# Attention inside an adaLN block on one core: value products and row sums moved to a fixed distance behind the scores, rotary products moved from VectorE to GpSimd

## The reference, cut to what matters

```python
h = layernorm(x) * (1 + ca) + sa
q = rmsnorm(h @ wq_a.T) @ wq_b.T          # 32 heads of 64 (nope) + 64 (rotary)
ckv, k_pe = split(h @ wkv_a.T)            # 32 latent columns, 64 rotary columns
k_nope, v = split(rmsnorm(ckv) @ wkv_b.T)
q_pe, k_pe = rope(q_pe), rope(k_pe)       # even * cos - odd * sin, odd * cos + even * sin
p = softmax(causal(q_full @ k_full.T * scale))
x = x + ga * ((p @ v) @ wo.T)
x = x + gb * ffn(layernorm(x) * (1 + cb) + sb)   # silu(gate) * up, then down
```

## Time and profile before

| | |
|---|---|
| median of 3 runs | 863.45 us (863.05 to 864.19) |
| the profiled execution, its own time | 862.18 us |
| its span, first to last instruction | 860.4 us |
| mean granted TensorE clock | 0.958 of full speed |
| busy: PE, DVE, POOL, ACT | 785.7, 533.1, 327.7, 271.5 us |
| first scores of window 0 | at 140.49 us |
| first scores of window 7 | at 560.01 us |
| first output product (L662) | at 615.58 us |

### The profile page before, as it was taken

One profiled execution on the slowest core, in us unless ns is written; L12 is line 12 of the kernel. 1 busy time (PEld: TensorE's weight loads), 2 busy tenths in 40 slices (PEclk: granted clock), 3 DMA queues, 4 the chain that ended last, 5 costly groups with the idle time before them and its releaser, 6 DMA issues.

```text
span 860.4 us, 10667 instructions
## 1 busy us (share of the span) xinstructions
PE 785.7 (91%) x3968; PEld 531.4 (62%) x3968; DVE 533.1 (62%) x836; ACT 271.5 (32%) x402; POOL 327.7 (38%) x199
## 2 busy tenths in 40 slices
PE   5659597999998999999999999999799899999997
PEld 5658254564664655656656655544487688886886
DVE  3354484896896896987978977756465333222342
ACT  2360002333433433433343333343344332221220
POOL 9220022374574574484564663524344100000111
PEclk9895687999999999999999999999899899999999
DMA  8300714306107007016034057046000032220011
GB/s 343 114 0 1 158 52 98 64 1 131 32 0 161 2 2 161 1 32 132 1 70 93 1 106 262 2 147 220 1 1 0 1 111 74 73 65 1 24 38 37
DMA packets 30275, 60.49 MB, mean 70 GB/s; under 512 B 4656, under 2 KB 16688, under 8 KB 28432
## 3 DMA queue, kind: packets, MB, share of 16 engines
q1 hardware_dynamic: 29024, 57.11, 24.8%
q10 hardware_dynamic: 1200, 2.69, 0.8%
HBM read 32.40 MB, written 2.10 MB: 40 GB/s over the span
## 4 chain that ended last, share of the span: by engine, by line
PE 60%; issue 12%; DVE 8%; POOL 7%; SPq 4%; DMA 4%; ACT 3%; POOLq 0%; ACTq 0%; DVEq 0%
PE PS L691 14%; PE PS L585 7%; PE PS L530 6%; PE PS L662 5%; PE PS L588 5%; PE PS L586 5%; PE PS L601 4%; POOL PR L1389 3%; DMA Q<-TQ 3%; SPq L386 2%; PE PS L459 2%; PE PS L521 2%; PE PS L534 1%; POOL RE L1354 1%; PE PS L512 1%
## 5 line engine op out<-in xcount | busy, mean ns | idle before, releaser
L817 ACT ACTIVATE PR<-PS 128x1024 f32<-128x1024 f32 (+1 forms) x144 | 132.9, 929 | 262.1 <-PE PS L588 183.5
L1085 DVE TENSOR_REDUCE NMa<-PS 128x1 f32<-128x512 f32 (+3 forms) x216 | 140.3, 665 | 44.4 <-PE PS L534 29.0
L530 PE MATMUL PS<-KH,Q 96*128 96x512 f32 (+3 forms) x384 | 132.2, 400 | 12.7 <-DMA Q<-TQ 10.6
L585 PE MATMUL PS<-Q,KH 128*128 128x512 f32 x288 | 132.5, 460 | 3.7 <-DMA Q<-NM 2.6
L1389 POOL TENSOR_TENSOR PR<-PR 128x1024 f32<-128x1024 f32 (+3 forms) x56 | 119.8, 2139 | 27.9 <-ACT PR L817 24.1
L691 PE MATMUL PS<-Q 128*128 128x512 f32 (+1 forms) x528 | 123.2, 396 | 5.1 <-DVE Q L1253 4.5
L691 PEld LDWEIGHTS PS<-Q 128*128 128x128 f32 (+1 forms) x528 | 99.3, 189 | 28.1 <-DVE Q L1253 4.7
L588 PE MATMUL PS<-Q,KH 128*128 128x512 f32 x288 | 114.6, 398 | 0.0
L586 PE MATMUL PS<-Q,KL 128*128 128x512 f32 x288 | 114.3, 397 | 0.0
L530 PEld LDWEIGHTS PS<-KH,Q 96*128 96x128 f32 x384 | 71.9, 196 | 49.2 <-issue 20.1
L585 PEld LDWEIGHTS PS<-Q,KH 128*128 128x128 f32 x288 | 56.1, 195 | 60.1 <-issue 28.2
(11 more groups left out here) (161 smaller groups left out, 1084.4 us busy)
## 6 DMA issues: line engine op xcount, KB each, us to landing
Q<-TQ SPq DMA_DIRECT2D x96, 256.0 KB, 5.0
PR<-in_wmod SPq DMA_DIRECT2D x6, 1024.0 KB, 7.2
RT<-in_wo SPq DMA_DIRECT2D x4, 1024.0 KB, 4.9
TQ<-in_wo SPq DMA_DIRECT2D x4, 1024.0 KB, 4.9
WI<-in_gate_w SPq DMA_DIRECT2D x10, 256.0 KB, 3.2
WI<-in_up_w SPq DMA_DIRECT2D x10, 256.0 KB, 3.6
DI<-in_down_w SPq DMA_DIRECT2D x10, 256.0 KB, 3.6
TQ<-in_x ACTq DMA_DIRECT2D x2, 1024.0 KB, 10.3
```

The costliest lines, as they stand in the source:

```text
L530: ins = pe.matmul(bank[:, i * w:(i + 1) * w], M.Q[0:KR, g % 2, 0, h0 + i, qt * P:(qt + 1) * P], M.KH[0:KR, lo:lo + w], start=(i == 0), sto ...
L585: pe.matmul(dst, M.KH[:, ks], M.Q[:, w % 2, 0, :, qs], start=True, stop=False)
L817: act.activation(tiles, banks, ACT.Exp).then_inc(S_.p, 1)
L1085: dve.tensor_reduce(dst, PS[:, bank_of(turn), 0:n * w].rearrange("p (h k) -> p h k", k=w), axis=AX.X, op=ALU.max, negate=True).then_inc(S_ ...
```

## The change

- **Order.** `UNITS` lists the 36 blocks of a window; every engine walks them with one table of side work per block. The values of a step come 3 blocks behind its last block and its sum 2 blocks behind, across the boundary of windows: the last two steps of a window are multiplied and added in the first blocks of the next one. `join` stands behind block 30 and `rows` behind block 32 of 0 to 35; before, both stood behind block 34, right behind the last part.
- **Sums.** DVE adds all four heads in one instruction; POOL adds none.
- **Rotary products.** For groups 1 to 7 ACT copies the even and odd projections out of their banks into RT, and POOL forms the four products (`rotate_even`, `rotate_odd`) and then the two sums. The latent's high part is copied by ACT for every group; DVE keeps the subtraction. ACT's copy waits until the preceding half has been combined (`re`).
- **Halves.** Q is laid out by query half, the maxima parts of half 0 come first (parts 0 to 10), and queries are sent by half: 4 transfers of 96 partitions for each half, 8 for a group where 12 were. Half 0 of group w+2 is sent in window w; half 1 of group w+1 at the start of window w. The key's columns are interleaved to match. In the prologue half 0 of group 1 is sent ahead of group 0's maxima.
- **Rows.** The score products use 97, 96 and 96 rows instead of 128, and the zero rows (six of seven memsets at the start) go.
- **Banks.** One `free` semaphore for each of the three banks, since ACT now frees some of them.

The diff, cut to its core:

```diff
-    return sorted(parts, key=lambda part: part[3] + part[4])
+    return sorted(parts, key=lambda part: (part[0] >= NS // 2, part[3] + part[4]))
...
+UNITS = [(s, i) for s in range(NSTEP) for i in range(units_of(s))]
+NUNIT = len(UNITS)
+VALUE_LAG, ADD_LAG = 3, 2
+
+
+def due(n, lag):
+
+    return [((n - lag) // NUNIT * -1, s) for s in range(NSTEP) if UNITS.index((s, units_of(s) - 1)) == (n - lag) % NUNIT]
+
+
+VALUES = [due(n, VALUE_LAG) for n in range(NUNIT)]
+SUMS = [due(n, ADD_LAG) for n in range(NUNIT)]
+LATE_VALUES = [s for n in range(NUNIT) for ago, s in VALUES[n] if ago]
+LATE_SUMS = [s for n in range(NUNIT) for ago, s in SUMS[n] if ago]
...
-        self.side, self.free = sem("side_filled"), sem("side_free")
+        self.side, self.free = sem("side_filled"), [sem(f"side_bank{b}_free") for b in range(3)]
...
-        self.q = [sem(f"q_sent{h}") for h in range(HG)]
+        self.q = [[sem(f"q_half{hf}_sent{h}") for h in range(HG)] for hf in range(2)]
...
-QUERY_PLACES = [(0.13, ("w", 0), 0.5), (0.14, ("w", 1), 0.15), (0.15, ("w", 2), 0.15), (0.25, ("even", 0), 1.2),
-                (0.28, ("odd", 0), 1.2), (0.36, ("lat", 0), 1.3), (0.40, ("split", 0), 0.0),
-                (0.54, ("even", 1), 1.2), (0.57, ("odd", 1), 1.2), (0.65, ("lat", 1), 1.3), (0.75, ("split", 1), 0.0)]
-WINDOW_US = 56.0
+QUERY_PLACES = [(0.10, ("w", 0), 0.5), (0.105, ("w", 1), 0.15), (0.11, ("w", 2), 0.15), (0.20, ("even", 0), 0.0),
+                (0.23, ("odd", 0), 0.0), (0.30, ("lat", 0), 0.7), (0.43, ("split", 0), 0.0),
+                (0.46, ("even", 1), 0.0), (0.49, ("odd", 1), 0.0), (0.56, ("lat", 1), 0.7), (0.70, ("split", 1), 0.0)]
+WINDOW_US = 57.0
...
-    begin, end = 0.1, 0.80
+    begin, end = 0.04, 0.84
     places = [(begin + (end - begin) * sum(cost[:k]) / sum(cost), ("part", k), cost[k]) for k in range(len(PARTS))]
-    return places + [(end + 0.01, ("join",), 0.1), (end + 0.02, ("rows",), 0.3)]
+    return places + [(end + 0.02, ("join",), 0.1), (end + 0.06, ("rows",), 0.3)]
...
-        places += [(0.09, ("den", 1), 0.7), (0.10, ("inv", 1), 0.8), (0.17, ("norm", 1), 0.0)]
+        places += [(0.15, ("den", 1), 0.7), (0.16, ("inv", 1), 0.8), (0.24, ("norm", 1), 0.0)]
+    places += [(0.42, ("den", 0), 0.7), (0.43, ("inv", 0), 0.8), (0.50, ("norm", 0), 0.0)]
+    places.sort(key=lambda x: x[0])
+    table = []
+    free = 0.0
+    for n in range(NUNIT):
+        place = (n + 1) / NUNIT
+        for ago, s in SUMS[n]:
+            if s in ADDS:
+                free = max(free, place) + (HG * width(s) / 960 + 0.07) / WINDOW_US
+        names = []
+        while places and (n == NUNIT - 1 or max(places[0][0], free - SLACK) <= place):
+            _, name, busy = places.pop(0)
+            names.append(name)
+            free = max(free, place) + busy / WINDOW_US
+        table.append(names)
     return table
...
-    def send_queries(g):
-        sp.wait_ge(S_.tl, 2 * (g + 1))
+    def send_queries(g, hf):
+        cols = slice(hf * QB, hf * QB + QB)
+        sp.wait_ge(S_.tl, 2 * g + hf + 1)
         if g > 1:
-            sp.wait_ge(S_.sc, NEXP * (g - 1))
+            sp.wait_ge(S_.sc, NEXP * (g - 2) + (FIRST_EXP[4] if hf == 0 else NEXP))
         for h in range(HG):
-            for b in range(3):
-                sp.dma_start(M.Q[b * 32:(b + 1) * 32, g % 2, :, h, :].bitcast(F32),
-                             M.TQ[h * 32:(h + 1) * 32, b, :, :].bitcast(F32)).then_inc(S_.q[h], 16)
+            sp.dma_start(M.Q[0:KR, g % 2, :, hf, h, :].bitcast(F32),
+                         M.TQ[h * L:(h + 1) * L, :, :, cols].bitcast(F32)).then_inc(S_.q[hf][h], 16)
...
-    sp.wait_ge(S_.pads, 7)
-    send_queries(0)
+    sp.wait_ge(S_.one, 1)
+    send_queries(0, 0)
+    send_queries(0, 1)
     load_weights(1)
     load_mod(5)
+    send_queries(1, 0)
     send_maxima(0)
-    for w in range(G - 1):
+    for w in range(G):
         if w < G - 2:
             load_weights(w + 2)
-        send_queries(w + 1)
+        if w < G - 1:
+            send_queries(w + 1, 1)
+        if w < G - 2:
+            send_queries(w + 2, 0)
         if w == G - 2:
-            for h in range(HG):
...
-        send_maxima(w + 1)
+        if w < G - 1:
+            send_maxima(w + 1)
...
-            pe.wait_ge(S_.free, turn - 2)
+            pe.wait_ge(S_.free[turn % 3], turn // 3)
...
-            pe.wait_ge(S_.q[h0 + i], 48 * (g + 1))
-            ins = pe.matmul(bank[:, i * w:(i + 1) * w], M.Q[0:KR, g % 2, 0, h0 + i, qt * P:(qt + 1) * P],
+            pe.wait_ge(S_.q[qt // 4][h0 + i], 16 * (g + 1))
+            ins = pe.matmul(bank[:, i * w:(i + 1) * w], M.Q[0:KR, g % 2, 0, qt // 4, h0 + i, qs],
...
-        pe.matmul(dst, M.KH[:, ks], M.Q[:, w % 2, 0, :, qs], start=True, stop=False)
-        pe.matmul(dst, M.KL[:, ks], M.Q[:, w % 2, 0, :, qs], start=False, stop=False)
         diagonal = i == 0 and s in DIAGONALS
-        ins = pe.matmul(dst, M.KH[:, ks], M.Q[:, w % 2, 1, :, qs], start=False, stop=not diagonal)
+        pe.matmul(dst, M.KH[0:KR + 1, ks], M.Q[0:KR + 1, w % 2, 0, qb, :, qs], start=True, stop=False)
+        pe.matmul(dst, M.KL[0:KR, ks], M.Q[0:KR, w % 2, 0, qb, :, qs], start=False, stop=False)
+        ins = pe.matmul(dst, M.KH[0:KR, ks], M.Q[0:KR, w % 2, 1, qb, :, qs], start=False, stop=not diagonal)
...
-        for s in range(NSTEP + 1):
-            if s < NSTEP:
-                for i in range(units_of(s)):
-                    scores(w, s, i)
-                    for name in TABLES[w].get(("s", s, i), []):
-                        side(of_window(w, name))
-            if s == NSTEP:
-                for name in TABLES[w]["last"]:
-                    side(of_window(w, name))
-            if s > 0:
-                values(w, s - 1)
-                for name in TABLES[w].get(("v", s - 1), []):
-                    side(of_window(w, name))
-        for name in TABLES[w]["end"]:
-            side(of_window(w, name))
+        for n, (s, i) in enumerate(UNITS):
+            scores(w, s, i)
+            for ago, before in VALUES[n]:
+                if ago <= w:
+                    values(w - ago, before)
+            for name in TABLES[w][n]:
+                side(of_window(w, name))
+    for s in LATE_VALUES:
+        values(G - 1, s)
     denominator(G - 1, 1)
...
+    def queries_copied(kind, g, hf):
+        turn = TURN[(kind, g, hf)]
+        act.wait_ge(S_.side, turn + 1)
+        act.wait_ge(S_.re, 2 * (2 * g + hf))
+        act.activation(M.RT[:, ("even", "odd").index(kind), :], PS[:, bank_of(turn), :], ACT.Copy).then_inc(
+            S_.free[turn % 3], 1)
+
+    def latent_high(g, hf):
+        turn = TURN[("lat", g, hf)]
+        cols = slice(hf * 512, hf * 512 + 512)
+        if g > 0:
+            for h in range(HG):
+                act.wait_ge(S_.q[hf][h], 16 * g)
+        act.wait_ge(S_.side, turn + 1)
+        act.activation(M.TQ[:, 2, 0, cols], PS[:, bank_of(turn), :], ACT.Copy).then_inc(S_.lh, 1)
 
...
-                    side(of_window(w, name))
-            if s == 4:
-                empty(w, 0)
-        for name in TABLES[w]["end"]:
-            side(of_window(w, name))
-        empty(w, 1)
+        for n, (s, i) in enumerate(UNITS):
+            e = FIRST_EXP[s] + i // 2
+            if i + 1 == EXPS[e][1] + EXPS[e][2]:
+                exponentials(w, e)
+            for ago, before in VALUES[n]:
+                if ago <= w and before in (3, NSTEP - 1):
+                    empty(w - ago, STEPS[before][0])
+            for name in TABLES[w][n]:
+                side(of_window(w, name))
+    empty(G - 1, 1)
...
-        if hf == 0 and g > 0:
-            for h in range(HG):
-                dve.wait_ge(S_.q[h], 48 * g)
-        dve.wait_ge(S_.side, turn + 1)
-        dve.tensor_copy(M.TQ[:, 2, 0, cols], PS[:, bank_of(turn), :]).then_inc(S_.lh, 1)
         dve.wait_ge(S_.lh, 2 * g + hf + 1)
         dve.tensor_tensor(M.TQ[:, 2, 1, cols], PS[:, bank_of(turn), :], M.TQ[:, 2, 0, cols].bitcast(F32),
-                          ALU.subtract).then_inc(S_.free, 1)
...
         if NADD * w + j > 0:
-            dve.wait_ge(S_.ae, NADD * w + j)
-        sums = M.SUM[qb][:, POOL_HEADS:, QB - wd:QB]
-        dve.tensor_tensor(sums, sums, M.slot(s)[:, POOL_HEADS:, 0:wd], ALU.add).then_inc(S_.ae, 1)
+            dve.wait_ge(S_.ad, NADD * w + j)
+        sums = M.SUM[qb][:, :, QB - wd:QB]
+        dve.tensor_tensor(sums, sums, M.slot(s)[:, :, 0:wd], ALU.add).then_inc(S_.ad, 1)
...
+        for n in range(NUNIT):
+            for ago, s in SUMS[n]:
+                if ago <= w and s in ADDS:
+                    add(w - ago, s)
+            for name in TABLES[w][n]:
+                side(of_window(w, name))
+    for s in LATE_SUMS:
+        add(G - 1, s)
...
-    pads = [(M.KH[KR:, :], 0.0), (M.KL[KR:, :], 0.0), (M.KH[KR:KR + 1, :], 1.0)]
-    pads += [(M.Q[KR:, par, hl], 0.0) for par in range(2) for hl in range(2)]
-    for n, (rows, value) in enumerate(pads):
-        if n > 0:
-            pool.wait_ge(S_.pads, n)
```

(47 more changed lines are left out.)

211 lines of the change are left out of this document (74 added, 137 removed).

## The result

The changed kernel takes 864.72 us (median of 20 runs, 862.1 to 869.78), the kernel before 862.55 in as many: a ratio of 1.0036 with an interval of 1.0024 to 1.0047. It is slightly slower. The forecast was 838 with a range of 822 to 856.

What follows compares the result with a forecast made beforehand. PE, busy 785.7 of 860.4 us, was taken as the bound, so only its idle could be won. Prologue -10.0, boundaries -12.9 and end -1.3 made -24.2, from 862.2 to 838 us; range 822 to 856.

Steps and rivals of the forecast that it cites:

- DVE is then [44.6 to 50.5]: DVE's load per window, 44.6 us if it never waits, 50.5 if it waits as before; under PE's 58.4.
- rival of the held side banks: In the windows, DVE's long sums outlast three banks' 3.5 us cover, costing PE 0.5 each at four sums; 851 us, chance 0.17.
- the fall by 5: DVE's load per window falls by 5 us, an argument against PE waiting on side banks.
- ACT waits for POOL: Rival: in the windows ACT's copy waits for POOL's rotary chain, delaying exponentials and stopping PE; 871 us, chance 0.10.
- Prologue: Before window 0: earlier sends and less DVE work, -10 us in all, bounds -5 and -16.
- the early half: Prologue: half 0 of group 0 is sent 6.4 us earlier, so group 1's weights land at about 102.1; -6.4 us.
- The stretch behind it: Prologue, 108.50 to 137.90: DVE falls to 19.4 us, PE's 25.46 then bounds it; -3.9 us.
- Boundaries: Window boundaries: PE's idle mostly goes, -9.8 in windows 1 to 5, -1.8 window 0, -1.3 window 6; -12.9 us.
- the 0.3 kept: Windows 1 to 5: PE idle still left after the change, 0.3 us a window, 1.5 in five.
- End: Window 7 loses 0.5 of idle, and one DVE add replaces POOL's adds behind it, -0.8; together -1.3 us.
- Faster transfers: Rival: sends naming 96 partitions double the 208 GB/s, so prologue weights land 7 us sooner; 831 us, chance 0.10.
- costed at nothing: Edits priced at 0, among them 96- and 97-row score products, with up to 3 us either way in the range.

Runs made afterwards that it cites:

- experiment 12: Kernel of experiment 5 with the first send of group 0 held until both query halves are ready; 856.21 us, 0.9935 of the kernel before.
- experiment 5: Changed kernel with the low part of half 1 moved from behind block 25 to behind block 28; 848.25 us, 0.9826 of the kernel before.
- Experiment 11: Kernel of experiment 5 with join and rows both behind the last block instead of 30 and 32; 899.23 us, 1.0443 of the kernel before.
- experiment 2: Changed kernel with 128 rows again in all score products, zero rows written again; 853.18 us, 0.991 of the kernel before.
- 1: Changed kernel with the low part's table entry one block later, which left ACT's and POOL's order as it was; 864.9 us, 1.0047 of the kernel before.
- experiment 10: Changed kernel with the low part behind block 28 and 128 rows in the score products, no filler; 839.46 us, 0.9737 of the kernel before.
- experiment 9: Changed kernel with the low part behind block 28, 128 rows and 14 unread filler products ahead of window 0; 837.86 us, 0.9716 of the kernel before.

## Why the prediction was wrong, point by point

**Two steps failed.** The first is "DVE is then [44.6 to 50.5] ... All are under PE's 58.4", with the rival of the held side banks at no more than 0.17. DVE's load came out inside these bounds, 49.55, but near the upper one: the fall by 5, which the prediction held against that rival, did not come (the sums took 21.3 us a window, where 16.5 stood, much of it waiting). And a mean doesn't tell where the long instructions meet. The prediction had worked out the very case ("behind L1360's 2.75, 5.0", against three banks' cover of 3.5) and then weighed it by load. The table repeats in every window, so a meeting that comes once comes six times: 59.18 instead of 61.23 is 10.3 us over windows 1 to 5, and there is a sixth wait in window 0. So this rival came true: it was priced at 12.9, as 0.5 us at each of four sums, and cost some 12.3, as one wait of 1.8 at one sum.

The Trainium skill, "SBUF - State Buffer", section Who interferes with whom, has the rule for it: a DVE instruction with two SBUF inputs and a GpSimd instruction that reads SBUF use one shared port pair, and whichever is issued first blocks the other. The traces agree: 4.53 us where POOL's instruction began first, 2.28 without it.

The second is an omission: no term of the sum stood for the clock in the windows; it was weighed for the prologue only. Before, it was down from 137 to 147.2; in the changed kernel from 127 to 154, and again 7 us in window 4 and 3 in window 5, behind the new wait. Window 0 is 69.14, and 56.71 with the collision and the idle mended. The 12.4 between them, less 2 for the collision, is some 10 us; the two later drops are 64.17 + 62.77 - 2 x 61.23 = 4.5 us. Collision and clock together, 12.3 + 10.4 + 4.5 = 27.2, are about the distance from the forecast. The rival "ACT waits for POOL" was refuted: ACT waited for PE and DVE alone, and its 25.82 us are the 25.8 forecast.

**The terms one by one.**

- Prologue, -10 forecast, -8.8 measured. DVE's wait for the weights ended at 100.45 instead of 108.47, 8.0 us earlier, where 6.4 stood. Of this the early half is 6.3, the term as forecast: so much later the wait ends in experiment 12. With both halves held back the weights still land 17.4 us after the first send where they took 18.7, and that send begins 0.5 earlier, which is the rest. The stretch behind it, forecast to lose 3.9 with DVE's load, lost 0.8 (31.25 for 32.02 us): PE and DVE wait for each other there (24.40 and 21.03 busy of 31.25), and the larger busy time isn't the length. The stated bounds of -5 and -16 don't follow from the bounds of the three terms, which add up to +2 and -14.
- Boundaries, -12.9 forecast. With the collision gone windows 1 to 5 take 295.9 (experiment 5), -7.65 where -9.8 stood. The idle fell below the 0.3 kept, to 0.1 a window; but PE's busy time, taken as unchanged at 58.43 to 58.51, is 59.1. That is the mis-sized term, 3.2 us over five windows, and 0.1 a window of it are the partial rows. Window 6 gave the 1.35 for which 1.3 stood. Experiment 11 shows that it is the head start of `join` and `rows` that hides the maxima.
- End, -1.3 forecast, -2.7 measured from window 7's first scores on. Only 1.0 of it lies ahead of the first output product (54.60 us for 55.57), where the forecast had its terms. The other 1.7 lies behind it, where the diff changes nothing: the clock was low from 618 to 623 there, and from 614 to 622 before. That part is luck.
- POOL: 25.0 forecast, 30.3 measured. One of the products takes 2.68 us on average and another 1.98 where L1376, never held off, takes 1.29; of POOL's work only the one low part reached PE:

```profile
L1378 POOL TENSOR_TENSOR RT<-RT,sin 128x512 f32<-128x512 f32 x10 | 26.8, 2682 | 0.8
L1388 POOL TENSOR_TENSOR TQ<-RE,TQ 128x1024 fp32r<-128x1024 f32 x10 | 24.2, 2416 | 23.2 <-ACT TQ L828 23.2
...
L1370 POOL TENSOR_TENSOR RT<-RT,cos 128x512 f32<-128x512 f32 x10 | 19.8, 1980 | 0.8
...
L1376 POOL TENSOR_TENSOR RT<-RT,cos 128x512 f32<-128x512 f32 x10 | 12.9, 1289 | 0.0
```

- "Faster transfers", at twice the rate, didn't come: the stretch from 90 to 100 us moved 233 GB/s where the earlier trace rows has 208, and the 1.3 us above is all that the 96-partition sends can have gained. By the rule of ports (the Trainium skill, "SBUF - State Buffer", section Door 1: The DMA port swizzle, by which the partitions of a transfer decide how many ports serve it) 96 partitions would have reached twice as many. Nothing of that size came while the source stays at 32 partitions; which side limits isn't tested.
- Rows 97 and 96 were "costed at nothing", 3 us either way. In the products they cost that, 0.1 us a window. What they cost is the clock's return: 11.7 us in experiment 2 against 1, 8.8 in experiment 10 against 5, and 1.6 with the filler (within the spread of those runs). That lies outside the 3 us.

The changed kernel with one table entry moved, 128 rows and the idle ahead of window 0 filled (experiment 9) reaches the 838 that was forecast for it as it stood. That it is the same number is partly luck. The profile has the prologue at -8.1 (forecast -10), windows 1 to 5 at -8.0 (-9.8), window 6 at -1.5 (-1.3) and the end at -2.2 (-1.3); window 0 gave -5.0 where -1.8 stood, about 3.3 of it because the low clock that the kernel before has there until 147.2 is gone, which stood in no term. The hidden boundary and the early half were read rightly; what was missing was the price of one coincidence and of a few microseconds of idle.
